# Two more blocks of o turned by VectorE instead of TensorE in a graph-convolution kernel

## The reference, cut to what matters

```python
def _L0_gnn_ref(x, d_list, U, Vt, weight, filt, bias):      # U = Vt = adj
    xw = x @ weight
    Vxw = Vt @ xw
    scale = jnp.sum(d_list * filt * d_list, axis=0)
    out = U @ (scale[:, None] * Vxw)
    return out + bias

def _L1_gnn_ref(X, A, W_in, W_out):
    def _message(X, A, W):
        deg = jnp.sum(A, axis=1, keepdims=True)
        return (A / jnp.where(deg > 0, deg, 1.0)) @ X @ W
    return _message(X, A, W_in) + _message(X, A.T, W_out)

x = _layernorm(x + _L0_gnn_ref(x, d_list, adj, adj, weight, filt, bias), axis=-1)
x = _layernorm(x + _L1_gnn_ref(x, adj, W_in, W_out), axis=-1)
```

## Time and profile before

| | |
|---|---|
| median of three runs | 738.88 us |
| lowest and highest | 738.81, 739.02 us |
| the profiled execution | 738.7 us, of which the span from first to last instruction is 736.9 us |
| mean granted TensorE clock | 0.997 |
| TensorE matmuls busy | 727.3 us, 99% of the span, 3296 instructions |
| VectorE busy | 581.2 us, 79%, 723 instructions |
| ScalarE busy | 511.7 us, 69%, 1304 instructions |
| GpSimd busy | 18.6 us, 3% |

### The profile page before, as it was taken

The page is one execution under the profiler, slowest core; times in us unless marked ns, Lnnn a source line. Parts: engine busy times, 40 slices in busy tenths (PEclk is TensorE's granted clock), DMA queues, the critical chain, the costliest instruction groups (busy, mean ns, idle before and its releaser), DMA issues.

```text
span 736.9 us, 9156 instructions
## 1 busy us (share of the span) xinstructions
PE 727.3 (99%) x3296; PEld 601.5 (82%) x3296; DVE 581.2 (79%) x723; ACT 511.7 (69%) x1304; POOL 18.6 (3%) x15
## 2 busy tenths in 40 slices
PE   8999999999999999999999999999999999999996
PEld 5888888888888888888888888888888888888885
DVE  5998977563735478888786778998888999899995
ACT  5888985744726364667474547999889888877772
POOL 1122200000000000000000000000000000000000
PEclk9999999999999999999999999999999999999998
DMA  8999995555545346776646459999989999999990
GB/s 343 424 426 422 426 414 190 194 217 217 193 159 195 145 169 229 261 271 266 226 174 255 156 220 385 384 385 389 367 327 390 388 363 385 379 350 354 347 366 29
DMA packets 35533, 217.02 MB, mean 295 GB/s; under 512 B 3617, under 2 KB 8481, under 8 KB 9761
## 3 DMA queue, kind: packets, MB, share of 16 engines
q1 hardware_dynamic: 35072, 215.79, 75.7%
q10 hardware_dynamic: 416, 0.66, 0.3%
HBM read 214.34 MB, written 2.10 MB: 294 GB/s over the span
## 4 chain that ended last, share of the span: by engine, by line
PE 96%; DMA 2%; DVE 1%; SPq 0%; ACT 0%; issue 0%; DVEq 0%
PE accA L663 14%; PE accA L668 14%; PE accA L673 14%; PE accB L663 12%; PE accB L668 12%; PE accB L673 12%; PE accC L673 6%; PE accC L668 6%; PE accC L663 6%; PE nat L696 3%; DMA raw<-in_adjT_b 2%; DVE lo L454 0%; PE nat L703 0%; SPq L281 0%; DVE rows L574 0%; ACT hi L330 0%
## 5 line engine op out<-in xcount | busy, mean ns | idle before, releaser
L454 DVE TENSOR_TENSOR lo<-raw,hi 128x2048 fp32r<-128x2048 f32 (+2 forms) x236 | 463.5, 1988 | 100.7 <-ACT hi L324 90.0
L324 ACT ACTIVATE hi<-raw 128x512 fp32r<-128x512 f32 x512 | 315.4, 621 | 72.0 <-DMA raw<-in_adjT_b 47.9
L663 PE MATMUL accA<-hi,x_hi 128*128 128x512 f32 x448 | 175.6, 392 | 1.7 <-ACT hi L330 1.7
L668 PE MATMUL accA<-hi,x_lo 128*128 128x512 f32 x448 | 174.4, 389 | 0.0
L673 PE MATMUL accA<-lo,x_hi 128*128 128x512 f32 x448 | 120.3, 389 | 0.0
L663 PE MATMUL accB<-hi,v_hi 128*128 128x512 f32 x256 | 100.1, 391 | 0.0
L663 PEld LDWEIGHTS accA<-hi,x_hi 128*128 128x128 f32 x448 | 84.1, 188 | 19.3 <-DVE x_lo L462 2.1
L668 PE MATMUL accB<-hi,v_lo 128*128 128x512 f32 x256 | 99.6, 389 | 0.0
L673 PEld LDWEIGHTS accA<-lo,x_hi 128*128 128x128 f32 x448 | 84.0, 188 | 17.8 <-DVE lo L454 0.4
L668 PEld LDWEIGHTS accA<-hi,x_lo 128*128 128x128 f32 x448 | 84.2, 188 | 17.0
L324 ACT ACTIVATION_READ_ACCUMULATOR hi<-raw 128x1 f32 x512 | 97.1, 190 | 0.0
(11 more groups left out here) (76 smaller groups left out, 468.1 us busy)
## 6 DMA issues: line engine op xcount, KB each, us to landing
raw<-in_adjT_b SPq DMA_DIRECT2D x137, 1024.0 KB, 4.9
raw<-in_adj_b SPq DMA_DIRECT2D x64, 1024.0 KB, 4.9
rows<-in_x_t SPq DMA_DIRECT2D x8, 256.0 KB, 10.6
out<-rows SPq DMA_DIRECT2D x7, 256.0 KB, 5.6
raw<-in_adjT_b ACTq DMA_DIRECT2D x1, 512.0 KB, 6.0
raw<-in_adjT_b SPq DMA_DIRECT2D x1, 512.0 KB, 6.8
out<-rows SPq DMA_DIRECT2D x1, 128.0 KB, 1.8
out<-rows ACTq DMA_DIRECT2D x1, 128.0 KB, 1.8
```

What stands on the lines that cost most here:

```text
L324: nc.scalar.activation(hi[slot][:, t], raw[slot][:, t], ACT.Copy, accum_out=to[:, TPB * K + t, C:C + 1]).then_inc(s_hi, 1)
L454: nc.vector.tensor_tensor(lo[slot][:, at], raw[slot][:, at], hi[slot][:, at], ALU.subtract).then_inc(s_lo, 1)
L663: nc.tensor.matmul(acc, r_hi[:, TPB * K + t], h[:, t], start=(first and t == 0), stop=False)
L668: nc.tensor.matmul(acc, r_lo[:, TPB * K + t], h[:, t], start=False, stop=False)
```

## The change

One constant is added, BY_PE = 2: TensorE turns o of that many blocks, 7 and 6. Blocks 5 and 4 are added in SBUF, to `part[:, I]` instead of to `turned`, and then turned by 16 VectorE transposes that read this buffer. A new semaphore, `s_ot`, counts them; `s_os` still counts the sums. VectorE waits for its own sum before the transposes. `x1_block` of 5 and 4 takes the form that 3 to 0 had. ScalarE's `save_y`, which writes y's part over `part[:, I]`, waits for the transposes of 5 and 4. TensorE's two calls of `turn_o` go, and the numbers of the later fills of `nat` are two lower.

```diff
+BY_PE = 2
@@ numbers of the later fills of nat
-            NAT_H[w_out_at[n]] = 2 * NB - LEAD + k
+            NAT_H[w_out_at[n]] = NB + BY_PE + k
@@ ScalarE
             def save_y(I):
                 act.wait_ge(s_rel, rank[last2[I]])
-                act.wait_ge(s_os, o_saved(I))
+                if LEAD <= I < NB - BY_PE:
+                    act.wait_ge(s_ot, NB - BY_PE - I)
+                else:
+                    act.wait_ge(s_os, o_saved(I))
@@ VectorE
             def o_sum(I):
                 u = 2 * NB - 1 - I
-                if I >= LEAD - 2:
+                if I >= NB - BY_PE - 2:
                     dve.wait_ge(s_n, u - 1)
...
                 dve.wait_ge(s_o, NB - 1 - I)
-                if I < LEAD:
-
-                    of = accB[:, I % 2].rearrange("p (t n) -> p t n", t=TPB)
-                    to = turned[:, u % 2].rearrange("p (t f) -> p t f", t=TPB)
-                    for a in range(0, P, 32):
-                        for b in range(0, P, 32):
-                            last = nc.vector.transpose(to[b:b + 32, :, a:a + 32], of[a:a + 32, :, b:b + 32])
-                    last.then_inc(s_os, 1)
-                    return
-                dve.wait_ge(s_os, o_saved(I) - 1)
-                nc.vector.tensor_tensor(turned[:, u % 2], accB[:, I % 2], part[:, I], ALU.add).then_inc(s_os, 1)
+                of = accB[:, I % 2]
+                if I >= LEAD:
+                    dve.wait_ge(s_os, o_saved(I) - 1)
+                    of = turned[:, u % 2] if I >= NB - BY_PE else part[:, I]
+                    nc.vector.tensor_tensor(of, accB[:, I % 2], part[:, I], ALU.add).then_inc(s_os, 1)
+                    if I >= NB - BY_PE:
+                        return
+                    dve.wait_ge(s_os, o_saved(I))
+
+                of = of.rearrange("p (t n) -> p t n", t=TPB)
+                to = turned[:, u % 2].rearrange("p (t f) -> p t f", t=TPB)
+                for a in range(0, P, 32):
+                    for b in range(0, P, 32):
+                        last = nc.vector.transpose(to[b:b + 32, :, a:a + 32], of[a:a + 32, :, b:b + 32])
+                last.then_inc(s_os if I < LEAD else s_ot, 1)
@@ VectorE
             def x1_block(I):
                 k = NB - 1 - I
-                if I < LEAD:
-                    dve.wait_ge(s_os, o_saved(I))
+                if I < NB - BY_PE:
+                    dve.wait_ge(s_os if I < LEAD else s_ot, o_saved(I) if I < LEAD else NB - BY_PE - I)
@@ TensorE
-                for I in range(NB - 3, LEAD - 1, -1):
+                for I in range(NB - 3, NB - BY_PE - 1, -1):
                     if n == last2[I] + (3 if I == NB - 3 else 2):
                         turn_o(I)
```

More of the change, by code:

```diff
@@ L79, in graph_kernel @@
         if n in w_out_at:
-            NAT_H[w_out_at[n]] = 2 * NB - LEAD + k
+            NAT_H[w_out_at[n]] = NB + BY_PE + k
         else:
-            NAT_Y[w_in_at[n]] = 2 * NB - LEAD + k
-    NAT_Y[NB - 1] = 4 * NB - LEAD - 1
+            NAT_Y[w_in_at[n]] = NB + BY_PE + k
+    NAT_Y[NB - 1] = 3 * NB + BY_PE - 1
     both = [n for n in range(N1, N2) if chunks[n][0] > chunks[n][1]]
@@ L153, in graph_kernel @@
     NAT_O = NB
+    NAT_2 = NB + BY_PE
     def o_saved(I):
@@ L238, in graph_kernel @@
         s_os = sem("o_taken")
+        s_ot = sem("o_with_part_turned")
         s_ty = sem("turned_y_ready")
@@ L355, in turn_h @@
                 act.wait_ge(s_rel, rank[last_z2[J]])
-                if NAT_H[J] < 2 * NB - LEAD + 2:
+                if NAT_H[J] < NAT_2 + 2:
                     act.wait_ge(s_x1, NB)
```

## The result

The changed kernel took 744.61 us (four runs, 744.37 to 744.74) against 738.88 before (738.81 to 739.02): a ratio of 1.0075, 95% interval 1.0063 to 1.0087. A second set of five runs gave 744.57 us, ratio 1.0073 (1.0059 to 1.0087). It is slower by 5.7 us.

A forecast was written before the change was run, and what follows sets the result against it. TensorE was taken as the bound, without slack until its tail. Waits of 2.94, 2.15 and 1.65 less 0.96 for the turns gave +5.8 us, forecast 744.6 us, range 742.3 to 746.0.

The forecast's parts named there:

- three late lo: At o(70), o(72) and o(74), TensorE waits for lo queued behind VectorE's new transposes; with the turns' saving, +5.8 us.
- TensorE is the bound, without slack behind: TensorE, busy 99% of the span, has no room until its tail, so waits put into it move the end.
- The turns, 0.96 us: Removing TensorE's turns of block 5 (0.49 us) and block 4 (0.47 us) takes 0.96 us off the path.
- The transposes, 5.20 us for 16 by the rows that read PSUM: Each of blocks 5 and 4 adds 16 VectorE transposes from SBUF, priced at 0.325 us each like those from PSUM.
- the two rivals that had it far lower: Transposes from SBUF are cheaper through both ports (742.6 us, chance 0.09) or overlap (740.4 us, chance 0.04).
- The first rival: Transposes read SBUF through both ports, saving 1.0 us for 16: +3.7, 742.6 us; chance 0.09.
- The chain: VectorE's steps from block 5's sum at 283.54 to low(74) at 315.04, fixed by durations alone, without waiting for TensorE.
- The waits: TensorE waits for lo 2.94 us at o(70), 2.15 at o(72) and 1.65 at o(74).
- The forecast's own addition: Profiled execution shifted from 738.7 to 744.5 us; the median of the runs lies 0.18 above it, stated as 744.6.
- the second rival: Transposes from SBUF overlap at a pitch of 0.197 us, 3.15 for 16: +1.7, 740.4 us; chance 0.04.
- the clock falls in the first wait: TensorE's clock drops to 1.2 GHz; absorbed before the second wait, up to +1.7 in the third, 746.3 us; chance 0.06.
- The cover holds: At low(70), low(72) and low(74), transposes cheap enough leave no wait: no slower or faster, 737.9 us; chance 0.03.

The follow-up runs named there:

- block 5 alone: Against the kernel before, VectorE turns only block 5 and TensorE keeps blocks 7, 6 and 4: median 742.80 us, ratio 1.0048.

## Why the prediction was right

744.6 us was forecast and 744.61 measured, by the mechanism forecast: three late lo, no later recovery. Step by step:

- **TensorE is the bound, without slack behind:** right; the whole difference is in the stretch up to o(74).
- **The turns, 0.96 us:** right, and isolated: -0.96 without the transposes.
- **The transposes, 5.20 us for 16 by the rows that read PSUM:** from SBUF 16 took 5.05, 303 ns each for 313 from PSUM before (312 in this trace):

```profile
L524 DVE STREAM_TRANSPOSE turned<-accB 32x128 f32<-32x128 f32 x64 | 20.0, 312 | 2.1 <-PE accB L683 1.2
L524 DVE STREAM_TRANSPOSE turned<-part 32x128 f32<-32x128 f32 x32 | 9.7, 303 | 0.5
```

  That is 0.15 less a block. The forecast turned on this price, and the two rivals that had it far lower fall: at 0.316 us each they neither overlap (a single one is 0.303) nor stream twice as fast. The Trainium skill, "VectorE: DVE Perf Modes", section "Why PSUM operands drop a tier", says that the two-port mode needs both read ports of SBUF, while PSUM has one for this engine. The first rival drew a gain for the transposes from it; this trace shows none, the two are 10 ns apart.
- **The chain:** low(70) was forecast for 289.49 and began at 289.49, low(71) 297.09 and 297.10, low(72) 305.24 and 305.10, low(74) 315.04 and 314.90. This execution began the sum 0.14 later, which hides the first block's 0.15.
- **The waits:** 2.94, 2.15 and 1.65 forecast; 2.87, 2.0 and 1.64 by the starts. The listed idle times, for which the forecast gave 2.9, 2.1 and 1.6, are 0.3 to 0.4 shorter, for the reason given above. o(76) was forecast for 323.80 and began at 323.72. Sum less the turns: +5.8 forecast, +5.56 in the profile. The two blocks' transposes were 0.30 too dear. Against that, a lo product was forecast to start 0.12 us after its low ends; it started about 0.05 after (291.83 against 291.78 for o(70)) but then took 0.13 longer, 0.06 more in all at o(74).
- **The last tenth is luck:** the term was 0.2 too large, and the medians differ by 5.73 where the profiles differ by 5.56. The profiled execution took 744.37, where 744.5 was forecast. The forecast's own addition was also 0.1 short: 744.5 and 0.18 are 744.7.
- **Slips in its sums:** 5.24 us for 16 is 0.328 each, not 0.325 (the chain itself uses 5.20 and 0.04), and +1.7 over 738.88 is 740.6, not the 740.4 of the second rival. Neither touches the forecast.
- **The rival "the clock falls in the first wait"** happened in some executions, and cost nothing here for the reason given, the slack at the second wait. Where that slack is missing (block 5 alone) it cost 1.53 us in the execution that was profiled. One detail was wrong: it does not fall during the wait but about 1 us after TensorE has resumed.
- **"The cover holds"** was wrong for this order, and right in kind: moved behind the lo that is due, the same 32 transposes are covered.

## What to carry to other kernels

Moving work off the bounding engine gains what it cost there (0.96 us) and loses what the receiving engine lacks before its next delivery. Read that cushion from the timeline at the very place: 3.0 us at low(70), against 5.35 of new work. A busy share of 79% for the span says nothing of it. Then carry the receiving engine's chain on until it waits for the other again, because lateness is handed on: the two blocks together cost 1.3 us more than the sum of each alone, and repairing two let a third fail. The cure is to place each step by when its result is needed, not by the block that it belongs to.

## What the runs showed of the hardware that I had not expected

A wait of 2.9 us on TensorE (2.58 listed idle) is followed by a fall of the granted clock to 1.2 GHz in some executions and not in others of the same kernel: one profile of block 5 alone has it and one has not, and the same holds for the changed kernel. Three of four runs of block 5 alone, and its later one, took the longer time. The fall comes after the resumption (near 292.5 in the run shown, TensorE resuming at 291.7) and costs 1.53 us there; in the changed kernel, where a second wait follows some 15 us later, it cost nothing. And a lo product that had to wait takes 0.13 us longer for its four matmuls (1.20 for 1.07), on top of the wait.
